# Moving the skip term between the weighted copies on ACT, with one decay semaphore per batch parity

## The chip, the core and the metric

The kernel runs on one core of a Trainium2 chip. PE (TensorE) does matmuls and transposes, DVE (VectorE) elementwise work and the scan, ACT (ScalarE) activations, POOL (GpSimd) elementwise work, and SP issues most DMAs. Each engine works through its own queue in order and waits for the others by semaphores. The metric is the device time of one execution in microseconds (us), lower is better.

## The reference

For 8 batches of 512 rows and 128 channels: a layer norm with a modulation from a condition, a Mamba block, a gated residual, a second layer norm, and a mixture of 8 experts (two of them weighted per row) beside a shared expert, with a second gated residual. Cut to what matters here:

```
mod = silu(c) @ wmod                                  # six vectors per batch
h = layernorm(x) * (1 + ca) + sa
xc, z = split(h @ in_proj.T);  xb = silu(conv4(xc) + conv_b)
dt, B, C = split(xb @ x_proj.T);  delta = softplus(dt @ dt_w.T + dt_b)
h[t] = h[t-1] * exp(delta[t] * A) + (delta[t] * xb[t]) * B[t]      # 16 states, 512 steps
y = (h * C).sum(states) + xb * D                      # xb * D is the skip term
x = x + ga * ((y * silu(z)) @ out_proj.T)
h = layernorm(x) * (1 + cb) + sb
x = x + gb * (shared(h) + sum_e w_e(h) * expert_e(h))  # w: softmax, top 2
```

## The kernel before

One batch is 256 inner channels (two groups q of 128 partitions) by 512 steps. The 16 states are cut into 16 units per batch (`UN`), each of one q and two states, so a unit is a tile of 128x1024 floats. For unit u of batch b:

- ACT `decays(b, u)` (L764 to L776): two activations exp(delta * A) into a ring of 8 decay tiles
- DVE `scan_input(b, u)` (L1067): B * du into PSUM, then `scan(b, u)` (L1076): the recurrence over 1024 columns into a ring of 4 states
- POOL `readout(b, u)` (L403): state * C. It is paced: it also waits for `input_done` of unit u + 1
- PE `y_add(b, u)` (L477): 8 transposes that accumulate the states into y in PSUM. Unit 15 is read out and added in the next slot, and so are the `y_add` of 13 and 14.

`pipeline` runs slots. In the slot of batch b, four batches are in work: b in its scans, a = b - 1 in its tail (gate, output projection, second norm, experts), n = b + 1 in its head (convolution, projections, delta), m = b + 2 in its first norm. The setup slot is the one with n = 0 and no b and a. Each engine has a function `slots(b, a, n, m)` whose order of calls is its queue.

What stands around the change in a slot with all four:

- DVE: after the scan of unit 7, `make_delta(n)` (L1040 to L1049) finishes delta and counts `delta_done`. After the scan of unit 12, `delta_x(n)` (L1056) makes `du` = xb * delta in place over xb. It waits for `skip_done`, because the skip term reads xb from the same tile. Behind it stand the scan inputs of units 13, 14 and 15, and in the next slot `gate_y` (L1086), `residual` and `split_h2` (L1180, `h_lo`).
- ACT: after the gelus of the experts (L903), `softplus_log(n)` (L846), the decays of b's unit 8, then a loop over j = 0 to 6: the decays of b's unit 9 + j, at j = 4 and 5 the decays of n's units 0 and 1, at j = 6 `h_rows(m)` (L784), and the weighted copies `mix_scaled(a, j)` (L869, four activations from PSUM). Then n's decays of unit 2, `mix_scaled(a, 7)`, `acc_rows(a)` (L876), `skip_term(n)` (L804, two activations, D * xb) and n's decays of units 3 to 5. After that comes the next slot, with the convolution's silu (L795).
- PE: `down(a, j)` (L633) and `mix_add(a, j)` (L643) alternate with b's `y_add`; `mix_add(a, j)` waits for the copy j. After `mix_add(a, 7)` come `y_add(b, 12)`, `acc_transpose(a)` (L652), and in the next slot `conv_in(n, 0)` (L504), `y_add` 13, `conv_in(n, 1)`, `y_add` 14 and 15, `x_proj`, `g_transpose`.

In the setup slot ACT ends with `z_gate(0)` (L813), for which PE's next `conv_in` waits.

`scan(b, u)` waits until the one semaphore `decay_done` has reached 16 b + u + 1. In ACT's order the decays of n's units 0 and 1 stand ahead of b's units 14 and 15, and count on the same semaphore.

Of the kernel before, what the change touches and what calls it, by code (L numbers as in the profile page):

```python
# [39 lines left out]
UN = 2 * CH  # L40
# [20 lines left out]
def adaln_mamba_moe_kernel(nc, x, in_proj_w, conv_w, conv_b, x_proj_w, dt_w, dt_b, a_log, d_skip,  # L61
# [4 lines left out]
    with ExitStack() as ctx:  # L66
# [3 lines left out]
        def sem(name):  # L70
            return ctx.enter_context(nc.semaphore(name))
# [128 lines left out]
        skip_done = sem("skip_done")  # L200
        du_done = sem("du_done")

        decay_done = sem("decay_done")
        input_done = sem("input_done")
        scan_done = sem("scan_done")
        read_done = sem("readout_done")
# [43 lines left out]
        def units_after(b, u):  # L250

            return b.i * UN + (u + 1)

        def unit(u):

            return u // (2 * Q), (u // 2) % Q, NU * (u % 2)
# [467 lines left out]
        def _(act):  # L724
# [19 lines left out]
            def load_silu_table(n):  # L744


                if not (isinstance(n.i, int) and n.i == 0):
                    act.wait_ge(silu_table, n.i)
                nc.scalar.activation(table_scratch[:, 0:1], eps_tile[:, 0:1],
                                     ACT.Silu).then_inc(silu_table, 1)  # L750
# [13 lines left out]
            def decays(b, u):  # L764

                pair, q, first = unit(u)
                r = u % DECAY_RING
                if u == 0:
                    act.wait_ge(delta_done, Q * b.i + Q)
                if not (isinstance(b.i, int) and b.i == 0 and u < DECAY_RING):  # L770
                    act.wait_ge(scan_done, units_after(b, u - DECAY_RING))
                for s in range(NU):
                    k = pair * NG + first + s
                    last = nc.scalar.activation(decay[:, r, s, 1:L], delta[:, b.p, q, 1:L], ACT.Exp,  # L774
                                                scale=a_neg[:, q, k:k + 1])
                last.then_inc(decay_done, 1)  # L776

            def h_rows(n):
                act.wait_ge(xT_done, n.i + 1)
# [8 lines left out]
            def x_silu(n, q):  # L788
                if q == 0 and not (isinstance(n.i, int) and n.i < 2):

                    act.wait_ge(input_done, (n.i - 1) * UN)
                if q == 0 and n.i == 0:
                    act.wait_ge(set_ev, EV_VEC)
                act.wait_ge(conv_done, Q * n.i + q + 1)
                nc.scalar.activation(du[:, n.p, q, :], A[q], ACT.Silu,  # L795
                                     bias=vec[:, ROW_CONVB + q:ROW_CONVB + q + 1]
                                     ).then_inc(xb_done, 1)

            def skip_term(n):

                act.wait_ge(delta_done, Q * n.i + Q)
                for q in range(Q):
                    act.wait_ge(xb_done, Q * n.i + q + 1)
                    nc.scalar.activation(skip[:, q, :], du[:, n.p, q, :], ACT.Identity,  # L804
                                         scale=vec[:, ROW_D + q:ROW_D + q + 1]).then_inc(skip_done, 1)

            def z_gate(n):
                if not (isinstance(n.i, int) and n.i < 2):
                    act.wait_ge(gT_done, n.i - 1)
                zs = z_silu[:, n.p, :, :].rearrange("p t c -> p (t c)")  # L810
                for j in range(2):
                    act.wait_ge(z_done, 2 * n.i + j + 1)
                    nc.scalar.activation(zs[:, j * 512:(j + 1) * 512], A[j],  # L813
                                         ACT.Silu).then_inc(zs_done, 1)

            def bcdt_rows(n):
                act.wait_ge(xproj_done, n.i + 1)
                if not (isinstance(n.i, int) and n.i == 0):
                    act.wait_ge(bc_stored, n.i * 16)
                    act.wait_ge(dt_done, Q * n.i)  # L820
                nc.scalar.activation(bcdt[:, :], MISC[0:2 * NS + R, :], ACT.Copy).then_inc(bcdt_done, 1)

            def softplus_relu(n, q):
                act.wait_ge(dt_done, Q * n.i + q + 1)
                nc.scalar.activation(delta[:, n.p, q, :], A[q], ACT.Relu,
                                     bias=vec[:, ROW_DTB + q:ROW_DTB + q + 1]).then_inc(sp_relu, 1)

            def softplus_abs(n, q, b):
                if b:
                    act.wait_ge(skip_acc, b.i + 1)  # L830
                act.wait_ge(dt_done, Q * n.i + q + 1)
                nc.scalar.activation(skip[:, q, :], A[q], ACT.Abs,
                                     bias=vec[:, ROW_DTB + q:ROW_DTB + q + 1]).then_inc(sp_abs, 1)

            def softplus_exp(n, a):
                act.wait_ge(sp_abs, Q * n.i + Q)
                if a:
                    act.wait_ge(oproj_done, a.i + 1)
                elif n.i > 0:
                    act.wait_ge(delta_done, Q * n.i)  # L840
                nc.scalar.activation(g_soft[:, :, :], skip[:, :, :], ACT.Exp,
                                     scale=-1.0).then_inc(sp_exp, 1)
# [6 lines left out]
            def g_rows(a, n):  # L849
                act.wait_ge(g_tr, a.i + 1)  # L850
                act.wait_ge(delta_done, Q * a.i + 2 * Q if n or isinstance(a.i, int) and a.i < B - 1
                            else Q * B)
                nc.scalar.activation(g_soft[:, :, :].rearrange("p q t -> p (q t)"), G_ROWS,
                                     ACT.Copy).then_inc(g_done, 1)

            def att_rows(a):
                act.wait_ge(oproj_done, a.i + 1)
                nc.scalar.activation(turned[:, :], OUTP, ACT.Copy,
                                     scale=gateT[:, 0, bass.ds(a.i, 1)]).then_inc(att_done, 1)
# [46 lines left out]
            def slots(b, a, n, m):  # L906
                if n:
                    load_silu_table(n)
                    x_silu(n, 0)
                    x_silu(n, 1)  # L910
                    bcdt_rows(n)
                if a:
                    g_rows(a, n)
                    att_rows(a)
                for q in range(Q):
                    if n:
                        softplus_relu(n, q)
                        softplus_abs(n, q, b)
                if n and n.i > 0:
                    z_gate(n)  # L920
                if n:
                    softplus_exp(n, a)
                if a:
                    load_exp_table(a)
                    h2_rows(a)
                if b:
                    decays(b, AHEAD)
                    decays(b, AHEAD + 1)
                if a:
                    router_e(a)  # L930
                    load_gelu_table(a)
                    for k in range(M_UP):
                        gelu(a, k)
                    weights_out(a)
                if n:
                    softplus_log(n)
                if b:
                    decays(b, AHEAD + 2)
                for j in range(DOWNS - 1):
                    if b:  # L940
                        decays(b, AHEAD + 3 + j)
                    if n and j in (4, 5):
                        decays(n, j - 4)
                    if m and j == 6:
                        h_rows(m)
                    if a:
                        mix_scaled(a, j)
                if n:
                    decays(n, 2)
                if a:  # L950
                    mix_scaled(a, DOWNS - 1)
                    acc_rows(a)
                if n:
                    skip_term(n)
                    for u in range(3, AHEAD):
                        decays(n, u)
                    if n.i == 0:
                        z_gate(n)

            pipeline(act, slots, setup)  # L960


        @block.vector
        def _(dve):
# [104 lines left out]
                                        ALU.mult).then_inc(input_done, 1)  # L1069

            def scan(b, u):
                dve.wait_ge(decay_done, units_after(b, u))
                if not (isinstance(b.i, int) and b.i == 0 and u < STATE_RING):
                    dve.wait_ge(yacc_done, units_after(b, u - STATE_RING))
                dve.wait_ge(input_done, units_after(b, u))
                nc.vector.tensor_tensor_scan(  # L1076
                    state[:, u % STATE_RING, :, :].rearrange("p n t -> p (n t)"),
                    decay[:, u % DECAY_RING, :, :].rearrange("p n t -> p (n t)"),
                    IN.rearrange("p n t -> p (n t)"), 0.0, ALU.mult, ALU.add).then_inc(scan_done, 1)
# [194 lines left out]
```

## Time and profile before

| | us |
|---|---|
| median of 3 runs | 754.61 |
| lowest, highest | 753.71, 760.47 |
| profiled execution | 761.24 |
| its span, first to last instruction | 759.5 |
| mean granted TensorE clock in it | 0.891 |
| busy PE, DVE, ACT, POOL | 625.6, 589.6, 497.0, 322.5 |

The profiled execution is a single one and lies at the upper end of the three timed runs. All rows below are of it. A row of a timeline gives the start and the duration in us, the engine and line, the output and inputs, and how many like instructions it holds. In square brackets stand the idle time of the engine ahead of it and what ended that. Starts of merged neighbours can overlap a little, since an engine begins an instruction before the last one has fully drained. A granted clock of 1.00 is full speed (2.4 GHz), 0.50 is half (1.2 GHz).

### The profile page before, as it was taken

What the parts mean: (1) busy time and instruction counts of PE and PEld (TensorE: products, weight loads), DVE (VectorE), ACT (ScalarE), POOL (GpSimd) and SP (SyncE); (2) the same over time, 40 slices, a digit from 0 to 9 for tenths busy, and PEclk for the clock granted to TensorE, in tenths of its full rate; (3) what the DMA queues carried; (4) which work ended last, traced back from release to release, by engine and by line L of the source; (5) the groups of instructions that cost most, each with busy time, mean ns of one, the idle gap of its engine ahead of it and who ended that gap; (6) DMA issues with size and microseconds to landing.
All of it is one profiled execution on the core that took longest, in us unless ns stands there. A gap on an engine that the chain in (4) does not pass through costs nothing.

```text
span 759.5 us, 9754 instructions
## 1 busy us (share of the span) xinstructions
PE 625.6 (82%) x3662; PEld 490.2 (65%) x3662; DVE 589.6 (78%) x669; ACT 497.0 (65%) x893; POOL 322.5 (42%) x172
## 2 busy tenths in 40 slices
PE   6547369997899969996999969996999758996897
PEld 4214245877477945885577936795487747795776
DVE  4477999796989969896989788996988699794300
ACT  3557643899278954898288945897289904871363
POOL 1025455353644635443543545443534464563000
PEclk9868559999799989998899989997999957997599
DMA  6503334133431325123421423231422343210000
GB/s 199 224 1 128 110 139 169 57 110 113 138 129 57 112 81 186 55 112 112 154 113 55 157 90 134 80 123 76 148 105 95 128 138 112 81 46 15 0 1 15
DMA packets 26369, 77.80 MB, mean 102 GB/s; under 512 B 2817, under 2 KB 17234, under 8 KB 18130
## 3 DMA queue, kind: packets, MB, share of 16 engines
q1 hardware_dynamic: 25842, 76.75, 27.9%
q8 instruction: 29, 0.48, 0.2%
q10 hardware_dynamic: 480, 0.43, 0.2%
q14 instruction: 18, 0.15, 0.1%
HBM read 74.55 MB, written 2.62 MB: 102 GB/s over the span
## 4 chain that ended last, share of the span: by engine, by line
PE 58%; ACT 23%; DVE 9%; issue 5%; POOL 3%; DMA 1%; POOLq 0%; DVEq 0%; ACTq 0%
PE psum L477 11%; PE psum L633 11%; PE psum L504 8%; ACT decay L774 6%; ACT gT_mix L869 4%; PE psum L601 4%; DVE state L1076 3%; PE psum L602 3%; PE psum L603 3%; POOL state L403 3%; ACT h L903 3%; DVE psum L1067 3%; PE psum L643 2%; PE psum L549 2%; PE psum L528 2%
## 5 line engine op out<-in xcount | busy, mean ns | idle before, releaser
L403 POOL TENSOR_TENSOR state<-state,bc 128x1024 f32<-128x1024 f32 x128 | 302.4, 2363 | 355.8 <-DVE psum L1067 354.8
L1076 DVE TENSOR_TENSOR_SCAN state<-decay,psum 128x1024 f32<-128x1024 f32 x128 | 292.2, 2283 | 19.5 <-PE psum L477 4.2
L477 PE MATMUL psum<-ident,state 128*128 128x128 f32 x1024 | 149.3, 296 | 73.2 <-POOL state L403 73.2
L477 PEld LDWEIGHTS psum<-ident,state 128*128 128x128 f32 x1024 | 129.2, 153 | 94.9 <-POOL state L403 81.3
L774 ACT ACTIVATE decay<-delta,a_neg 128x511 f32<-128x511 f32 x256 | 167.1, 728 | 30.7 <-DVE state L1076 28.5
L1067 DVE TENSOR_TENSOR psum<-bc,du 128x1024 f32<-128x1024 f32 x128 | 157.6, 1231 | 5.0 <-DVE state L1076 0.5
L633 PE MATMUL psum<-down_w,h 128*128 128x128 f32 x1024 | 125.3, 276 | 0.0
L633 PEld LDWEIGHTS psum<-down_w,h 128*128 128x128 f32 x1024 | 119.2, 192 | 6.1 <-issue 6.1
L903 ACT ACTIVATE h<-psum,vec 128x512 f32<-128x512 f32 x144 | 97.0, 688 | 15.6 <-PE psum L603 14.2
L869 ACT ACTIVATE gT_mix<-psum,w 128x128 f32<-128x128 f32 x256 | 74.0, 387 | 25.0 <-PE psum L643 17.6
L504 PE MATMUL psum<-h_sb,conv_in_wT 128*128 128x512 f32 x128 | 66.5, 671 | 17.0 <-ACT z_silu L813 17.0
L601 PE MATMUL psum<-h_hi,up_hi 128*128 128x512 f32 x144 | 61.5, 427 | 2.2 <-ACT h L903 1.3
L602 PE MATMUL psum<-h_lo,up_hi 128*128 128x512 f32 x144 | 58.3, 405 | 0.0
L603 PE MATMUL psum<-h_hi,up_lo 128*128 128x512 f32 x144 | 58.3, 405 | 0.0
L504 PEld LDWEIGHTS psum<-h_sb,conv_in_wT 128*128 128x128 f32 x128 | 27.3, 224 | 46.9 <-issue 46.8
L795 ACT ACTIVATE du<-psum,vec 128x512 f32<-128x512 f32 x16 | 11.0, 689 | 63.7 <-PE psum L504 63.7
L1056 DVE TENSOR_TENSOR du<-du,delta 128x1024 f32<-128x1024 f32 x8 | 9.8, 1222 | 39.6 <-ACT skip L804 39.6
L643 PE MATMUL psum<-ident,gT_mix 128*128 128x128 f32 x256 | 38.7, 274 | 1.9 <-ACT gT_mix L869 1.3
L601 PEld LDWEIGHTS psum<-h_hi,up_hi 128*128 128x128 f32 x144 | 28.0, 195 | 9.7 <-ACT h L903 2.8
L603 PEld LDWEIGHTS psum<-h_hi,up_lo 128*128 128x128 f32 x144 | 28.0, 194 | 6.9
L643 PEld LDWEIGHTS psum<-ident,gT_mix 128*128 128x128 f32 x256 | 29.8, 142 | 3.7 <-ACT gT_mix L869 3.7
L602 PEld LDWEIGHTS psum<-h_lo,up_hi 128*128 128x128 f32 x144 | 28.2, 196 | 5.5
(137 smaller groups left out, 633.1 us busy)
## 6 DMA issues: line engine op xcount, KB each, us to landing
bc<-bc_rows SPq DMA_DIRECT2D x64, 1024.0 KB, 4.7
x_sb<-_attn_hidden_states_dram SPq DMA_DIRECT2D x9, 256.0 KB, 2.8
out_dram<-out_sb SPq DMA_DIRECT2D x8, 256.0 KB, 2.4
x<-_attn_hidden_states_dram SPq DMA_DIRECT2D x7, 256.0 KB, 3.1
h<-in_L_ffn_rw_dram SPq DMA_DIRECT2D x1, 1024.0 KB
bc_rows<-rows SPq DMA_DIRECT2D x8, 64.0 KB, 1.6
h<-in_L_wmod_dram ACTq DMA_DIRECT2D x1, 384.0 KB
h<-in_L_attn_in_proj_w_dram SPq DMA_DIRECT2D x1, 256.0 KB, 4.4
```

Source lines behind the costliest of these rows:

```text
L403: pool.tensor_tensor(state[:, u % STATE_RING, :, :], state[:, u % STATE_RING, :, :], bc[:, pair % BC_RING, 1, first:first + NU, :], ALU.mu ...
L477: last = nc.tensor.matmul(Y[q][:, t * P:(t + 1) * P], state[:, u % STATE_RING, s, t * P:(t + 1) * P], ident[:, :], start=False, stop=(u in ...
L504: last = nc.tensor.matmul(A[q], conv_in_wT[:, q, k, :], h_sb[:, k:k + L], start=(k == 0), stop=(k == KC - 1))
L601: nc.tensor.matmul(bank, high, h2_hi[:, :], start=True, stop=False)
L602: nc.tensor.matmul(bank, high, h2_lo[:, :], start=False, stop=False)
L603: nc.tensor.matmul(bank, low, h2_hi[:, :], start=False, stop=True).then_inc(up_done, 1)
L633: last = nc.tensor.matmul(A[j % 2][:, e * DM:(e + 1) * DM], h1[:, (group * EG + e) * HQ + q, ts], down_w[:, group * EG + e, q, :], start=( ...
L774: last = nc.scalar.activation(decay[:, r, s, 1:L], delta[:, b.p, q, 1:L], ACT.Exp, scale=a_neg[:, q, k:k + 1])
L869: last = nc.scalar.activation(mix[:, j % 2, e, :], A[j % 2][:, e * DM:(e + 1) * DM], ACT.Copy, scale=w9[:, t, group * EG + e:group * EG + ...
L903: nc.scalar.activation(h1[:, m, :], UP_RING[m % 3], ACT.Gelu, bias=vec[:, bias:bias + 1]).then_inc(gelu_done, 1)
L1067: nc.vector.tensor_tensor(IN, bc[:, pair % BC_RING, 0, first:first + NU, :], du[:, b.p, q:q + 1, :].broadcast_to([P, NU, L]), ALU.mult).th ...
L1076: nc.vector.tensor_tensor_scan(state[:, u % STATE_RING, :, :].rearrange("p n t -> p (n t)"), decay[:, u % DECAY_RING, :, :].rearrange("p n ...
```

## The change

`skip_term(n)` is called in the loop at j = 3, behind the decays of b's unit 12 and ahead of `mix_scaled(a, 3)`, and no longer behind `acc_rows(a)`. There are two decay semaphores, chosen by the parity of the batch, and `scan(b, u)` waits on its own batch's for (b // 2) * 16 + u + 1. Nothing else differs.

```
-        decay_done = sem("decay_done")
+        decay_done = [sem(f"decay_done{p}") for p in range(2)]
...
-                last.then_inc(decay_done, 1)
+                last.then_inc(decay_done[b.p], 1)
...
                 for j in range(DOWNS - 1):
                     if b:
                         decays(b, AHEAD + 3 + j)
+                    if n and j == 3:
+                        skip_term(n)
                     if n and j in (4, 5):
                         decays(n, j - 4)
...
                     acc_rows(a)
                 if n:
-                    skip_term(n)
                     for u in range(3, AHEAD):
                         decays(n, u)
...
             def scan(b, u):
-                dve.wait_ge(decay_done, units_after(b, u))
+                dve.wait_ge(decay_done[b.p], (b.i // 2) * UN + u + 1)
```

ACT's queue in the first slot that has a tail (b = 1), from the decays of unit 11 on, before:

```order
L774 ACTIVATE decay<-delta,a_neg 128x511 x2
L869 ACTIVATE gT_mix<-psum,w 128x128 x4
L774 ACTIVATE decay<-delta,a_neg 128x511 x2
L869 ACTIVATE gT_mix<-psum,w 128x128 x4
L774 ACTIVATE decay<-delta,a_neg 128x511 x4
L869 ACTIVATE gT_mix<-psum,w 128x128 x4
```

and with the change:

```order
L774 ACTIVATE decay<-delta,a_neg 128x511 x2
L869 ACTIVATE gT_mix<-psum,w 128x128 x4
L774 ACTIVATE decay<-delta,a_neg 128x511 x2
L804 ACTIVATE skip<-du,vec 128x512 x2
L869 ACTIVATE gT_mix<-psum,w 128x128 x4
L774 ACTIVATE decay<-delta,a_neg 128x511 x4
L869 ACTIVATE gT_mix<-psum,w 128x128 x4
```

Here `gT_mix` is the tile of the weighted copies. The two skip activations now stand between the decays of unit 12 and the fourth copy; at the slot's end, behind `acc_rows` (L876), they are gone.

ACT's queue in the setup slot (batch 0), from the softplus logarithm to the z gate, before and with the change:

```order
 L846 ACT_TABLE_LOAD
 L846 ACTIVATE skip<-g_soft 128x1024
-L774 ACT_TABLE_LOAD
-L774 ACTIVATE decay<-delta,a_neg 128x511 x4
-L784 ACTIVATE h_sb<-psum,modT 128x512
-L774 ACTIVATE decay<-delta,a_neg 128x511 x2
-L804 ACTIVATE skip<-du,vec 128x512 x2
-L774 ACTIVATE decay<-delta,a_neg 128x511 x6
+L804 ACTIVATE skip<-du,vec 128x512 x2
+L774 ACT_TABLE_LOAD
+L774 ACTIVATE decay<-delta,a_neg 128x511 x4
+L784 ACTIVATE h_sb<-psum,modT 128x512
+L774 ACTIVATE decay<-delta,a_neg 128x511 x8
 L813 ACT_TABLE_LOAD
 L813 ACTIVATE z_silu<-psum 128x512 x2
```

The skip term stands first now, ahead of the load of the table for Exp.

## Rows read from the trace of the kernel before

**Rows 1.** The page: busy time of each engine (share of the span), instructions
```profile
PE 625.6 (82%) x3662; PEld 490.2 (65%) x3662; DVE 589.6 (78%) x669; ACT 497.0 (65%) x893; POOL 322.5 (42%) x172
```

**Rows 2.** Waits of DVE: us in total, times, longest us
```profile
DVE du L1056 <- ACT skip L804: 39.6, 7, 5.8
```

**Rows 3.** Timeline of DVE: setup, steady slots 1, 3, 4 and 6
```profile
42.50 1.23 DVE L1056 TENSOR_TENSOR du<-du,delta 128x1024 f32<-128x1024 f32 x1 [5.83 <-ACT skip L804]
...
187.60 1.23 DVE L1056 TENSOR_TENSOR du<-du,delta 128x1024 f32<-128x1024 f32 x1 [5.62 <-ACT skip L804]
...
329.33 1.29 DVE L1049 TENSOR_TENSOR delta<-delta,skip 128x512 f32<-128x512 f32 x2
...
347.07 2.29 DVE L1076 TENSOR_TENSOR_SCAN state<-decay,psum 128x1024 f32<-128x1024 f32 x1
355.00 1.23 DVE L1056 TENSOR_TENSOR du<-du,delta 128x1024 f32<-128x1024 f32 x1 [5.63 <-ACT skip L804]
...
373.70 1.23 DVE L1086 TENSOR_TENSOR gT_mix<-psum,z_silu 128x1024 f32<-128x1024 f32 x1 [1.12 <-PE psum L477]
...
390.35 1.17 DVE L1180 TENSOR_TENSOR h_lo<-h,h_hi 128x512 fp32r<-128x512 f32 x1 [1.82 <-ACT h_hi L884]
...
439.01 1.23 DVE L1056 TENSOR_TENSOR du<-du,delta 128x1024 f32<-128x1024 f32 x1 [5.71 <-ACT skip L804]
...
605.57 1.23 DVE L1056 TENSOR_TENSOR du<-du,delta 128x1024 f32<-128x1024 f32 x1 [5.39 <-ACT skip L804]
```

**Rows 4.** Timeline of POOL: readouts of units 12 and 15 of one batch
```profile
357.50 2.34 POOL L403 TENSOR_TENSOR state<-state,bc 128x1024 f32<-128x1024 f32 x1 [8.11 <-DVE psum L1067]
...
368.97 2.35 POOL L403 TENSOR_TENSOR state<-state,bc 128x1024 f32<-128x1024 f32 x1 [1.80 <-DVE psum L1067]
```

**Rows 5.** Timeline of PE: another slot's convolution, then 324 to 437
```profile
279.22 4.08 PE L504 MATMUL psum<-h_sb,conv_in_wT 128*128 128x512 f32 x8
...
324.74 1.95 PE L618 MATMUL psum<-h,down_w 128*128 128x512 f32 x4 [1.04 <-ACT rows L896]
...
359.89 1.97 PE L477 MATMUL psum<-ident,state 128*128 128x128 f32 x8 [6.97 <-POOL state L403]
...
362.51 5.10 PE L504 MATMUL psum<-h_sb,conv_in_wT 128*128 128x512 f32 x8
367.45 1.03 PE L477 MATMUL psum<-ident,state 128*128 128x128 f32 x8
368.32 3.60 PE L504 MATMUL psum<-h_sb,conv_in_wT 128*128 128x512 f32 x8
...
435.54 1.40 PE L643 MATMUL psum<-ident,gT_mix 128*128 128x128 f32 x8
```

**Rows 6.** Windows: length, busy PE, PEld, DVE, ACT, POOL, clock, DMA share, GB/s
```profile
299.00:354.00 55.00, 51.81 (x370) 45.45 (x368) 46.12 (x62) 50.04 (x95) 24.91 (x14) 1.00 0.30 114
...
359.80:362.60 2.80, 2.71 (x13) 2.71 (x14) 2.65 (x2) 2.75 (x4) 1.51 (x2) 0.50 0.00 0
362.60:367.70 5.10, 5.10 (x12) 2.22 (x12) 4.93 (x5) 0.07 (x1) 3.24 (x2) 0.71 0.23 62
```

**Rows 7.** Timeline of ACT: decays of unit 12, copy j = 3, skip
```profile
336.60 1.34 ACT L774 ACTIVATE decay<-delta,a_neg 128x511 f32<-128x511 f32 x2
338.96 1.14 ACT L869 ACTIVATE gT_mix<-psum,w 128x128 f32<-128x128 f32 x4 [1.01 <-PE psum L643]
...
353.54 1.32 ACT L804 ACTIVATE skip<-du,vec 128x512 f32<-128x512 f32 x2
```

**Rows 8.** Timelines of ACT, PE and DVE in the setup slot and behind it
```profile
33.29 1.28 ACT L774 ACT_TABLE_LOAD   x1
36.70 2.55 ACT L774 ACTIVATE decay<-delta,a_neg 128x511 f32<-128x511 f32 x4 [2.12 <-DVE delta L1049]
...
48.57 8.55 PE L504 MATMUL psum<-h_sb,conv_in_wT 128*128 128x512 f32 x16 [17.02 <-ACT z_silu L813]
...
63.87 2.29 DVE L1076 TENSOR_TENSOR_SCAN state<-decay,psum 128x1024 f32<-128x1024 f32 x1 [4.17 <-PE psum L477]
```

## Prediction of the changed kernel's time

> **What bounds the kernel now.** I began with the page's busy times [rows 1]: PE is busy 82% of the span, DVE 78%. Neither is full, so waits in a ring between engines must set the time. A steady slot of the batch pipeline repeats every 83.6 us, from (605.57 - 187.60) / 5 for the first and the last steady `du` multiply [rows 3]. The question is which wait ends last in a slot, so I read DVE's waits [rows 2]. The largest is `du` at L1056, which waits for ACT's skip term, 39.6 us in 7 waits. One of them (5.83 us, at 42.50) lies in the setup slot. The other six, 33.8 us in all or 5.6 each, lie in slots 1 to 6 [rows 2, 3].
>
> Then I followed one slot through the timelines. On DVE the scan of unit 12 ends at 349.36, `du` starts at 355.00 [rows 3]. On POOL, the readout of unit 12 is paced by the scan input of unit 13, which stands behind `du` on DVE, so it starts only at 357.50 [rows 4]. On PE it idles 6.97 us for that readout, until 359.89, so its last `mix_add` had ended at 352.92 [rows 5]. Behind this stand the transposed accumulation of unit 12, the transpose of the expert rows and both convolutions of the next batch. So the whole ring goes mix on PE, `acc_rows` and skip on ACT, `du` and the input on DVE, readout on POOL, PE again. The skip term is on it, although its inputs are old: the delta steps end at 330.62 [rows 3], and skip starts at 353.54 [rows 7]. Nothing but its place in ACT's queue makes it late.
>
> **What the change moves.** In a steady slot the two skip activations (1.32 us) go from behind `acc_rows` to behind the decays of unit 12, ahead of the fourth weighted copy (j = 3). Those decays end at 337.94; the delta steps, for which skip waits, had ended at 330.62, 7.3 us before. So skip runs at about 337.9 to 339.2 and `du`, ready at 349.37, waits for nothing. That takes 5.6 us off DVE's ring per slot.
>
> What it costs on ACT: the fourth copy started at 338.96 after 1.01 us of idle [rows 7]. Skip needs 1.2 to 1.3 us there (neighbours overlap by 0.1), so the copies behind are late by 0.2 to 0.3 us. From there to the end of the slot ACT's queue is full, and the delay reaches the last `mix_add`. PE then idles that much less ahead of unit 12, which is free as long as PE still has to wait there (below).
>
> **The new ring.** DVE from one `du` to being ready for the next: (439.01 - 5.71) - 355.00 = 78.30 us, and this contains waits for PE and ACT: 1.12 at the gate, 1.82 at `h_lo` [rows 3]. PE from the start of unit 12 to the end of its last `mix_add`: 436.94 - 359.89 = 77.05 [rows 5], plus 0.3 for the moved skip. The two rings meet at unit 12: PE may start it when the last `mix_add` has ended and when the readout has, which follows `du` by a fixed 4.9 us (355.00 to 359.86 [rows 3, 4]). Both are under 83.6, and DVE's is the longer by 78.30 - 77.35 = 0.95 us. So the next bound is DVE's ring, and PE still waits at unit 12, for about 1 us in place of 7.
>
> That shorter idle matters by itself. In the idle of 7 us the granted clock falls: it is 0.50 over 359.8 to 362.6, when PE works again, and comes back only during 362.6 to 367.7, whose mean is 0.71 [rows 6]. The work in between runs at half speed: 8 transposes 1.97 us against 1.03 at full clock, the first convolution 5.10 us (4.08 in another slot) against 3.60 [rows 5]. An idle of 1.04 us in the middle of a slot (ahead of 324.74) left the clock at 1.00 over the whole of 299 to 354 [rows 5, 6]. With about 1 us of idle I expect it to stay at its upper level, 2.4 GHz, so that the first convolution takes 3.6 us. PE could then save 3 us, but it gets less: unit 15 needs its readout, which is tied to DVE and ends at 371.32, 11.43 us after PE's unit 12 starts [rows 4, 5]. With 0.9 us of transposes it ends 12.35 us after, against 373.67 - 359.89 = 13.78 now (the gate at 373.70 starts on it [rows 3]). So 1.4 us. The gate's wait of 1.12 goes, and the rest shows at `h_lo`. DVE's ring becomes 78.30 - 1.4 = 76.9. In the slots where the convolution took only 4.08 us the ring was shorter already by about as much, so they end near 77 as well.
>
> On this clock the Trainium skill (TensorE: Matmul & The Clock Gate, Part 1) says that the clock gate is at 4/8 after idling and 8/8 after sustained work, which is the 0.50 and 1.00 of the trace. Its warning that the change-over varies from run to run agrees with the first convolution's 4.08 and 5.10 us; by that rule alone a part of the gain could be missing in some slots, which is the first rival below.
>
> **The setup slot pays.** For batch 0 the order on ACT was table load (33.29, while ACT waited for the delta steps), decays, skip, decays, table load, z gate. Now skip is first and waits for delta; the built order has the Exp table load behind it. The load of 1.28 us no longer lies in the wait that ends at 36.70, and all of ACT's work behind it, up to the z gate, comes 1.3 us later [rows 8]. PE's second convolution waits 17.02 us for that gate, and DVE's scan at 63.87 waits 4.17 us for PE [rows 8], so this 1.3 us is on the path. DVE gets its `du` sooner there (42.50 now [rows 3]), which only lengthens that wait. Beside it, the Trainium skill (ScalarE: Activation LUTs, Table sets) says that cheap functions are in every table set, so Identity needs no load of its own; the built order agrees, as in it no load stands ahead of skip, before or now.
>
> In slot 0 `du` waited for nothing. Skip will wait there for the delta steps and hold back the decays of unit 13, which are needed some 20 us later: nothing.
>
> The second edit, one decay semaphore per parity, adds no instruction. In the old count the decays of the next batch's units 0 and 1 counted for units 14 and 15 of this one; now the scan waits for the true ones. Unit 15's decays stand ahead of the old skip at 353.54 in ACT's queue, so with the 1.3 us of the moved skip they have ended by 354.9 at the latest [rows 7]. Unit 15's scan in the new order has `du`, three inputs and two scans ahead of it from 349.4 on, 1.2 + 3 x 1.2 + 2 x 2.3 = 9.4 us, so it starts at 358.8 or later [rows 3]: a margin of 4 us at least, so nothing.
>
> **The sum.** Slot 1: 5.6. Five rings at 83.6 - 76.95 = 6.65: 33.2. Setup: -1.3. Slot 7 and the tail: no convolution stands there, and a gain from the clock lies between 0 and 1.5 us; I take nothing. Together 37.5 us. The profiled execution has 761.24 us (span 759.5), so 723.7 on its own ground. It lies 6.6 us over the median of 754.61, and on the median's ground that would be 717.1. The first convolution's duration, 4.08 us in one slot and 5.10 in another [rows 5], is a kind of spread that the new order removes: over six slots up to 6 us. I count about half of the 6.6 as such. So about 720.5.
>
> **Rivals.**
> - *The clock still falls.* For: it fell in the idle of 7 us [rows 6], and my 1 us is the small difference of two long rings. Against: the 1.04 us idle did not do it. Then the gain is that of the waits alone, 33.8 - 1.3 = 32.5: 728.7 on the profile's ground, 722 on the median's.
> - *ACT stalls at the new place* (the other side). If the delta steps end later than the decays of unit 12, skip blocks the copies j = 3 to 7, the decays of 13 to 15 and `h_rows` behind it, and PE behind those. Now the margin is 7.3 us. A lateness beyond it would first eat PE's 1 us of idle and then 1:1 each slot. If the delta steps come L us later against ACT than now, the time is 720.5 + 6 x (L - 8.3): 747 us (1% under before) at L = 12.7, 762 us (1% over) at 15.2. For it: DVE becomes the bounding engine. Against: the delta steps and ACT's decays both hang on the same scans, so they move together.
> - *The change does nothing*: excluded if the trace is right, since `du` names skip as its last releaser in all seven waits, and the built order has moved it.
>
> **Numbers.** A measurement of this kernel can tell about 1% (7.5 us) from no change. My forecast 0.77, the clock falling 0.13: both are faster by over 1%, 0.90. ACT stalls so that 1% is not reached 0.06; slower by over 1% 0.04. The range goes from 714 (the median's ground with 1.5 us at the tail and 1.5 for the rest) to 729 (waits alone on the profile's ground).
>
> **What would show it.** DVE `du` has no wait for skip in slots 1 to 6; skip starts before the fourth copy; PE's idle ahead of unit 12 is 0.5 to 1.5 us, its releaser still POOL; the granted clock at the first convolution is 1.00 and it takes 3.6 us; `du` repeats every 77 us; the z gate of setup is 1.3 us later. It would be wrong if PE's idle has gone and the ring is over 78 us (then ACT's copies bound it), or if ACT waits for the delta steps ahead of skip in steady slots.

## The result, and the profile after

The changed kernel takes 724.47 us (median of 4, 722.56 to 725.67), beside 755.97 for the kernel before (753.71 to 760.47). The medians lie 31.5 us apart. The ratio, taken from the means, is 0.957, with a 95% interval of 0.952 to 0.963, so 4.3% less. The profiled execution took 722.56 us, with a span of 720.8 and a mean granted clock of 0.930 (0.891 before).

The page's first part, its chain by engine, and the waits of DVE (us in total, times, longest), where [rows 1, 2] stood:

```profile
PE 608.0 (84%) x3662; PEld 475.5 (66%) x3662; DVE 587.9 (82%) x669; ACT 495.3 (69%) x893; POOL 322.4 (45%) x172
...
DVE 38%; PE 36%; ACT 12%; issue 7%; POOL 5%; DMA 1%; DVEq 0%; POOLq 0%; ACTq 0%
```

```profile
DVE h_lo L1181 <- ACT h_hi L884: 17.4, 8, 3.5
...
DVE du L1057 <- ACT skip L804: 1.5, 1, 1.5
```

The 39.6 us that `du` waited for skip are 1.5 us, all in the setup slot. DVE is now the largest engine on the chain, where PE was before (58%, DVE 9%). Of the timelines, one slot of DVE, POOL and PE, and two rows of ACT from the slot behind it, the answers to [rows 3, 4, 5, 7]:

```profile
334.01 2.29 DVE L1077 TENSOR_TENSOR_SCAN state<-decay,psum 128x1024 f32<-128x1024 f32 x1
336.22 1.20 DVE L1057 TENSOR_TENSOR du<-du,delta 128x1024 f32<-128x1024 f32 x1
...
338.69 2.35 POOL L403 TENSOR_TENSOR state<-state,bc 128x1024 f32<-128x1024 f32 x1 [2.37 <-DVE psum L1068]
...
341.09 1.09 PE L477 MATMUL psum<-ident,state 128*128 128x128 f32 x8 [1.14 <-POOL state L403]
342.02 0.60 PE L652 MATMUL psum<-ident,h 128*128 128x128 f32 x4
342.46 3.60 PE L504 MATMUL psum<-h_sb,conv_in_wT 128*128 128x512 f32 x8
...
352.58 1.09 PE L477 MATMUL psum<-ident,state 128*128 128x128 f32 x8 [1.33 <-POOL state L403]
...
402.13 1.34 ACT L804 ACTIVATE skip<-du,vec 128x512 f32<-128x512 f32 x2
403.36 1.14 ACT L869 ACTIVATE gT_mix<-psum,w 128x128 f32<-128x128 f32 x4
```

`du` follows the scan of unit 12 at once. PE idles 1.14 us ahead of unit 12 where it idled 6.97, and the first convolution takes 3.60 us. So the slot looks as forecast. But not every slot does. Two steady slots have a longer wait at `h_lo`, 3.46 and 3.31 us in place of 1.83. The timelines of DVE and PE and two windows (length, busy PE, PEld, DVE, ACT, POOL, granted clock, DMA share, GB/s) show the first of them:

```profile
208.80 2.70 PE L512 MATMUL psum<-z_wT,h_sb 128*128 128x256 f32 x8
...
286.63 1.89 PE L512 MATMUL psum<-z_wT,h_sb 128*128 128x256 f32 x8
...
215.96 0.69 DVE L1181 TENSOR_TENSOR h_lo<-h,h_hi 128x512 fp32r<-128x512 f32 x1 [3.46 <-ACT h_hi L884]
...
195.00:206.00 11.00, 8.66 (x42) 4.38 (x39) 10.76 (x7) 2.88 (x5) 6.18 (x3) 1.00 0.43 149
206.00:210.00 4.00, 4.00 (x14) 3.05 (x14) 3.81 (x12) 2.04 (x4) 3.52 (x3) 0.63 0.82 305
```

The granted clock falls in the middle of the slot: it is 1.00 up to 207 us and 0.50 over 207 to 210, and PE is busy in all of those 3 us. The fall comes just behind the two dt projections (L528, matmuls that contract 8 rows). `z_proj` (L512) takes 2.70 us in this slot and 3.21 in the other, in place of 1.89, and its silu, `h_hi` and `h_lo` follow late. I call this a dip below.

Where the 38.7 us between the two profiled spans (759.5 and 720.8) lie, by the starts of `du`: the first steady one came at 187.60 and comes at 180.19, 7.4 us sooner; five rings fell from 417.97 to 388.49 us (to 568.68), 29.5 us; the rest fell from 153.9 to 152.1 us. The medians, 31.5 us apart, are less apart than the two profiles; the part on the prediction comes back to this.

### The profile page after: what moved, and what is told of

Same layout as the page of the kernel before. It is cut to its first block, busy times and chain, and to the rows that moved or that the text cites. A ratio compares the mean times of both kernels' runs of the same rounds, so it can differ in the third digit from the quotient of the medians.

```text
span 720.8 us, 9754 instructions
## 1 busy us (share of the span) xinstructions
PE 608.0 (84%) x3662; PEld 475.5 (66%) x3662; DVE 587.9 (82%) x669; ACT 495.3 (69%) x893; POOL 322.4 (45%) x172
## 4 chain that ended last, share of the span: by engine, by line
DVE 38%; PE 36%; ACT 12%; issue 7%; POOL 5%; DMA 1%; DVEq 0%; POOLq 0%; ACTq 0%
DVE state L1077 17%; DVE psum L1068 12%; PE psum L633 6%; PE psum L477 6%; POOL state L403 4%; PE psum L504 3%; PE psum L549 2%; ACT h L903 2%; PE psum L528 2%; PE psum L522 2%; PE psum L512 2%; ACT decay L774 2%; PE psum L601 2%; PE psum L542 1%; PE psum L603 1%
## 5 line engine op out<-in xcount | busy, mean ns | idle before, releaser
L477 PE MATMUL psum<-ident,state 128*128 128x128 f32 x1024 | 145.7, 290 | 45.6 <-POOL state L403 45.6
L477 PEld LDWEIGHTS psum<-ident,state 128*128 128x128 f32 x1024 | 125.0, 150 | 68.4 <-POOL state L403 52.8
L504 PE MATMUL psum<-h_sb,conv_in_wT 128*128 128x512 f32 x128 | 60.3, 617 | 18.7 <-ACT z_silu L813 18.7
L504 PEld LDWEIGHTS psum<-h_sb,conv_in_wT 128*128 128x128 f32 x128 | 24.4, 200 | 44.6 <-issue 44.6
L643 PE MATMUL psum<-ident,gT_mix 128*128 128x128 f32 x256 | 38.7, 274 | 3.8 <-ACT gT_mix L869 3.8
L795 ACT ACTIVATE du<-psum,vec 128x512 f32<-128x512 f32 x16 | 11.0, 688 | 39.6 <-PE psum L504 39.6
L853 ACT ACTIVATE g_soft<-psum 128x1024 f32<-128x1024 f32 x8 | 8.2, 1028 | 32.4 <-PE psum L542 32.4
```

Of the source, the lines that this page charges most:

```text
L477: last = nc.tensor.matmul(Y[q][:, t * P:(t + 1) * P], state[:, u % STATE_RING, s, t * P:(t + 1) * P], ident[:, :], start=False, stop=(u in ...
L504: last = nc.tensor.matmul(A[q], conv_in_wT[:, q, k, :], h_sb[:, k:k + L], start=(k == 0), stop=(k == KC - 1))
```

## The experiments

All timings are medians, and a ratio is to the kernel before as timed beside that run. For each profile I read the five rings of `du`, from the first to the last steady slot, and the dips in six steady slots (a `z_proj` over 2.5 us, or where that isn't read, `h_lo` waiting over 3.2 us):

| kernel | us | mean ring | dips of 6 |
|---|---|---|---|
| before | 755 to 760 | 83.59 | 1 |
| changed | 724.47 | 77.70 | 2 |
| changed, again | 724.85 | 77.69 | 2 |
| semaphores alone | 755.84 | 83.29 | 0 |
| setup order kept | 722.05 | 77.68 | 2 |
| skip ahead of acc_rows | 748.24 | 81.87 | 0 |
| before, 50 transposes in the idle | 758.72 | 83.77 | 4 |
| before, unit 12 unpaced | 762.37 | 83.82 | 3 |
| setup kept, short idles filled | 724.24 | 78.35 | 4 |
| skip's work twice | 724.88 | 77.66 | 2 |
| 8 transposes between the dt projections | 725.44 | 77.90 | 0 |
| 8 transposes ahead of them | 727.83 | 78.58 | 2 |
| unit 0 between them | 722.80 | 77.62 | 0 |
| 3 transposes between them | 720.29 | 77.35 | 0 |

The first eight runs were to tell apart two theories, A and B, that both say that the waits carry the gain, and differ on what the clock adds.

### The changed kernel again

> The changed kernel once more, as the yardstick of this group. The two theories are: (A) the six removed waits of du for the skip term carry the gain (5.6 us each, 33.8 us less 1.3 us in the setup slot), and TensorE's clock adds up to 1 us per slot; (B) the waits alone carry it, the clock gives nothing on balance, since a dip that went from the first convolution can come back elsewhere in the slot. Both expect 722 to 726 us here; A expects rings of du of 77.0 us where no stretch of the slot lies at half clock, B expects a mean ring of 78 us.

Measured 724.85 us, ratio 0.957 (0.952 to 0.961) to its own kernel before, mean ring 77.69, with dips in slots 5 and 6 (in slots 2 and 6 the first time). The rings without a dip are 77.0 (one is 77.4), as A has it; the mean is near that of B.

### The semaphores alone

```
-        decay_done = sem("decay_done")
+        decay_done = [sem(f"decay_done{p}") for p in range(2)]
-                last.then_inc(decay_done, 1)
+                last.then_inc(decay_done[b.p], 1)
-                dve.wait_ge(decay_done, units_after(b, u))
+                dve.wait_ge(decay_done[b.p], (b.i // 2) * UN + u + 1)
```

> The kernel before with the second edit alone, two decay semaphores by the batch's parity. Both theories: no instruction is added and unit 15's decays have long ended when its scan starts, so the time is that of the kernel before within 0.5% (752 to 759 us), and du still waits 5.6 us for skip in six slots. A theory by which the semaphores matter (the scan waits longer for the true decays, or less because the counts are separate) expects more than 5 us of difference.

Measured 755.84 us beside 756.16, ratio 1.000 (0.996 to 1.004). The second edit costs and brings nothing in time that this can tell, 0.4% either way. The move alone on the one semaphore was not tried, because it would have a race: decays of the next batch count for unit 14 before unit 14's own are written. In the kernel before, `du` waited for the skip term, which stands behind all decays of the batch on ACT, and this wait was what ordered the scans of units 14 and 15 behind their decays. The move takes that order away, so it needs the second edit.

### Batch 0's skip term at its old place

```
-                    if n and j == 3:
+                    if n and a and j == 3:
                         skip_term(n)
...
                 if n:
+                    if not a:
+                        skip_term(n)
                     for u in range(3, AHEAD):
```

> The changed kernel, but batch 0's skip term in the setup slot stands at its old place, behind the decays. If the Exp table load behind the moved skip (1.28 us) is on the path there, the z gate comes 1.3 to 1.4 us earlier against the delta steps than in the changed kernel, and the time falls by about 1.3 us, 0.2%, which a profile shows better than the times. If that stretch is covered, the time is the same and DVE waits as long for PE at its first stall.

ACT's timeline in the setup slot, first of the changed kernel, then of this one:

```profile
35.81 1.33 ACT L804 ACTIVATE skip<-du,vec 128x512 f32<-128x512 f32 x2 [3.42 <-DVE delta L1050]
37.16 1.28 ACT L774 ACT_TABLE_LOAD   x1
38.46 2.56 ACT L774 ACTIVATE decay<-delta,a_neg 128x511 f32<-128x511 f32 x4
...
46.59 1.28 ACT L813 ACT_TABLE_LOAD   x1
```

```profile
32.76 1.28 ACT L774 ACT_TABLE_LOAD   x1
36.16 2.55 ACT L774 ACTIVATE decay<-delta,a_neg 128x511 f32<-128x511 f32 x4 [2.12 <-DVE delta L1052]
...
45.51 1.28 ACT L813 ACT_TABLE_LOAD   x1
```

From the end of the delta steps (the first activation behind the wait) to the z gate's load it is 46.59 - 35.81 = 10.78 us in the changed kernel and 45.51 - 36.16 = 9.35 here: 1.4 us, the load in the open. The time, 722.05 beside 724.85, points the same way, but single runs of either spread over 4 us, so the 1.4 rests on the profile. How much of it reaches the end is open: behind the gate, PE's convolution takes 9.23 us in one profile and 9.78 in the other. The Trainium skill (ScalarE: Activation LUTs, What ACT_TABLE_LOAD costs) gives a load about 1.28 us and a drain of about 1.38 beside it. The load of 1.28 is what the rows show; the drain is not to be seen here, since the decays start 1.30 us after the load does (37.16 and 38.46).

### The skip term one step earlier only

```
-                    if n and j == 3:
-                        skip_term(n)
...
                 if a:
                     mix_scaled(a, DOWNS - 1)
+                if n:
+                    skip_term(n)
+                if a:
                     acc_rows(a)
```

> The changed kernel with the skip term between the last weighted copy and acc_rows, so only 1.4 us earlier than in the kernel before. It asks whether the time follows the skip term's place 1:1. If the ring through du bounds (A and B), du waits about 4.1 us in place of 5.6, each of six slots is 1.4 to 1.5 us shorter, and with the setup slot's 1.3 us the time is 755 - 8.7 + 1.3 = 748 us (745 to 751). If the gain came from taking ACT's work out of the end of the slot, it would be that of the kernel before; if any place ahead of acc_rows does, 724.

Its waits of DVE:

```profile
DVE du L1058 <- ACT skip L804: 30.9, 7, 5.8
```

Less the setup slot's 5.8 us that is 25.1 us in six slots, 4.2 each (5.6 before). The time is 748.24 beside 756.16, ratio 0.988 (0.985 to 0.992): 7.9 us. The wait fell by 8.7 us. I had added 1.3 us for the setup slot wrongly: in this kernel batch 0's order is the old one. The ring through `du` follows the place of the skip term nearly 1:1, which a gain from mere rearrangement at the end of the slot would not.

### PE's idle filled, skip left where it was

```
+                    if a and b and n and u == UN - 3:
+                        fill(a, 50)
                     if b:
                         y_add(b, u - 1)
```

> The kernel before, with 50 transposes of the identity on PE in its idle of 7 us ahead of unit 12's accumulation (their result is never used); skip stays where it was. It measures the clock by itself. By A the first convolution takes 3.6 us in all slots, PE reaches unit 15 as early as POOL allows, and the ring of du falls from 83.6 to about 82.6, so 6 us in all (747 to 751 us). By B the clock falls elsewhere in the slot in its place, and the time is that of the kernel before within 2 us.

Rows of its PE timeline:

```profile
268.23 5.62 PE L573 MATMUL psum<-ident 128*128 128x128 f32 x50
275.37 1.09 PE L477 MATMUL psum<-ident,state 128*128 128x128 f32 x8 [1.52 <-POOL state L403]
...
276.74 3.60 PE L504 MATMUL psum<-h_sb,conv_in_wT 128*128 128x512 f32 x8
...
299.08 2.75 PE L512 MATMUL psum<-z_wT,h_sb 128*128 128x256 f32 x8
```

The first part of A came true: the convolution takes 3.60 us, and rings without a dip are 82.8 us (187.66 to 270.47, 439.76 to 522.60), where 82.6 was expected. But in that same slot the clock then fells `z_proj`. Four of six steady slots dip, a ring with one is 83.9 to 84.8, and the mean is 83.77. The time is 758.72, ratio 1.001 (0.998 to 1.005): nothing gained, as B says (it is 2.3 us over the 756.38 beside it, where B allowed 2). In the kernel before, five of six steady slots had no dip, nor had any in the two other kernels whose clock falls at the start of each slot. So here a clock kept up at the start of the slot went with more dips some 20 us later. That the one brings the other is not shown: in slot 1 of both this kernel and the one before, the first convolution is slow (5.70 and 5.63 us) and the slot dips all the same.

### PE's idle taken away, skip left where it was

```
-                        readout(b, u)
+                        readout(b, u, paced=u != 12)
```

> The kernel before, with the readout of unit 12 no longer paced by the scan input of unit 13, so that POOL needn't wait for du; skip stays. It takes away PE's idle but not du's wait. By A and B the ring through du and skip hangs on PE's mix chain, so PE's 7 us are gone, the next accumulation (unit 13) waits for its readout instead, and the time falls only by what the clock and the earlier first convolution give, 1 to 2 us per slot (745 to 752 us). If PE's idle of 7 us were the cost by itself, this would bring most of the gain: 720 to 730 us.

```profile
357.40 1.04 PE L477 MATMUL psum<-ident,state 128*128 128x128 f32 x8
...
358.84 3.60 PE L504 MATMUL psum<-h_sb,conv_in_wT 128*128 128x512 f32 x8
368.17 1.97 PE L477 MATMUL psum<-ident,state 128*128 128x128 f32 x8 [5.73 <-POOL state L403]
369.93 5.39 PE L504 MATMUL psum<-h_sb,conv_in_wT 128*128 128x512 f32 x8
```

Unit 12 no longer waits; the idle stands one unit later, 5.73 us, the clock falls there, and now the second convolution is the slow one. 762.37 us, ratio 1.006 (1.003 to 1.010), so 6 us worse and not 4 to 11 better. The small gain I expected failed: the mean ring is 83.82, with three dips. These stand in slots whose second convolution was slow, so a fall early in the slot does not keep a later one away. In slot 0 there is a further cost, since the unpaced readout now runs beside a scan input on DVE:

```profile
106.71 3.37 DVE L1067 TENSOR_TENSOR psum<-bc,du 128x1024 f32<-128x1024 f32 x1
```

It takes 3.37 us in place of 1.23, and POOL's two readouts there take 5.66 in place of 2 x 2.34. The rest of the 6 us I didn't trace. That PE's idle by itself was not what cost the time is shown by both runs.

### The skip term's work twice

```
                     if n and j == 3:
+                        if a:
+                            (two activations, D * xb into a tile of their own, 496 columns each)
                         skip_term(n)
```

> The changed kernel with two more activations like the skip term (1.2 us, into a tile that nothing reads) right ahead of it in the slots with copies. PE has 1.1 us of idle left ahead of unit 12. If DVE's ring bounds the changed kernel, as forecast, ACT's added 1.2 us is eaten by that idle and the ring of du stays at 77.0 to 77.3 us: at most 2 us more in all. If ACT's copies bound it, the ring grows by 1.2 us in each of six slots: 7 us more.

```profile
326.28 1.31 ACT L949 ACTIVATE twin<-du,vec 128x496 f32<-128x496 f32 x2
327.48 1.34 ACT L806 ACTIVATE skip<-du,vec 128x512 f32<-128x512 f32 x2
...
341.99 0.65 PE L645 MATMUL psum<-ident,gT_mix 128*128 128x128 f32 x4 [1.37 <-ACT gT_mix L871]
342.63 1.09 PE L479 MATMUL psum<-ident,state 128*128 128x128 f32 x8
```

724.88 us, the time of the changed kernel, rings of 77.0 without a dip. The last copy comes later, and PE's idle ahead of unit 12 is used up. So ACT has 1.2 us to spare there, and it is DVE's ring that bounds the changed kernel. With PE's idle used up, one more microsecond on ACT in this stretch should be paid; that was not run.

### The short idles filled

The kernel of setup order kept, with 7, 9 and 5 transposes ahead of unit 12, of unit 15 and of `g_transpose`.

> The changed kernel with batch 0's skip at its old place, and with 7, 9 and 5 transposes of the identity in PE's three short idles of a slot (ahead of units 12 and 15 and of g_transpose; results never used). By A the dips of the clock in the middle of two slots go, all five rings of du are 77.0 us, and the time is 1.3 + 3 us under the changed kernel: 719 to 721 us. By B the dips have another cause and stay, and the time is that of the changed kernel less 1.3 us: 722 to 724 us.

724.24 us (719.57 to 727.79), four dips, mean ring 78.35. It is a miss for A. More work on PE in the idle places did not keep the clock up where it falls. This left open what precedes the fall. In the dips it comes at the end of the second dt projection or just behind it, so the next two runs put the same 8 transposes at two places around them.

### Eight transposes between the dt projections, and ahead of them

```
                 if a:
                     out_proj(a)
+                (ahead: fill(1, 8) here)
                 if n:
                     dt_proj(n, 0)
                 if a:
                     att_transpose(a)
+                (between: fill(1, 8) here)
                 if n:
                     dt_proj(n, 1)
```

> The e3 kernel (batch 0's skip at its old place) with 8 transposes of the identity on PE between the two dt projections, whose matmuls contract only 8 rows; the granted clock has fallen right behind them in some slots. It costs PE 0.9 us on its way to h_hi. By C (the fall hangs on what PE does there) no slot dips, h_lo never waits 3.3 us or more beyond the 0.9, and all rings of du are alike, 77.0 to 77.9 us. By B' (the fall hangs on something else, a matter of chance at that place) 2 to 4 of six slots still dip, and the time is 1 to 5 us over e3's.

> The control to it: the same 8 transposes ahead of the first dt projection, so the same 0.9 us at nearly the same place, with the two dt projections as close together as before. By C dips stay in 2 to 4 of six slots; by B' this and the run with the transposes between the projections are alike.

Between: no dip in six steady slots, rings of 77.6 to 78.2 us (C had said up to 77.9), times within 1.1 us of each other (724.50 to 725.60). Ahead: two dips, 727.83 us. Same work, same number of instructions, same cost of 0.9 us on the way to `h_hi`; only the place differs. None of six against two of six is thin by itself, and the next two runs add to it. Windows of the run with them ahead, from 1.2 us before `z_proj` in a slot with a dip, and of the run with 3 between (below), from the start of `z_proj`:

```profile
287.00:291.00 4.00, 4.00 (x16) 3.50 (x15) 3.96 (x13) 1.76 (x3) 1.57 (x3) 0.57 0.38 147
```

```profile
286.00:290.00 4.00, 4.00 (x31) 3.69 (x30) 4.00 (x6) 3.08 (x5) 1.32 (x3) 1.00 0.39 160
```

PE counts as busy for all of both windows, and the clock is 0.57 in one and 1.00 in the other. Nor is it the DMA traffic at this step, an obvious rival: its share is up to 1.02 in 1 us of the first, but in the run with 3 between it is 0.93 and 1.01 over 285 to 287, with the clock at 1.00.

### Needed work between them, and a smaller dose

The first moves `y_add(b, 0)` from behind the second dt projection to ahead of it; the second is the run with 8 transposes between, with 3.

> The e3 kernel with PE's accumulation of unit 0 (8 full transposes, needed work) moved from behind the second dt projection to between the two. By C, which the two runs with 8 transposes between and ahead of the projections bore out, no steady slot dips: z_proj takes 1.89 us in all. The second projection is 0.9 us later and half of that is covered by ACT, so rings of du are 77.4 to 77.6 us, and the time is 719.5 to 722. If only added transposes help, z_proj takes 2.7 us or more in some slots.

> As the run with 8 transposes between the dt projections, but 3. It asks how much is needed. By C with a small dose: no dips, rings of du 77.3 us, 719 to 721 us. If 3 are too few, some slots show z_proj at 2.7 us or more and the time is e3's, 722 to 724 us.

```profile
283.07 0.66 PE L556 MATMUL psum<-ident,h 128*128 128x128 f32 x4
283.56 0.49 PE L573 MATMUL psum<-ident 128*128 128x128 f32 x3
283.99 1.12 PE L528 MATMUL psum<-rows,small_w 8*128 8x512 f32 x2
285.04 1.09 PE L477 MATMUL psum<-ident,state 128*128 128x128 f32 x8
285.97 1.89 PE L512 MATMUL psum<-z_wT,h_sb 128*128 128x256 f32 x8
```

No dip in either. With unit 0 between, 722.80 us, 0.8 over what was expected: its rings of 77.6 us carry 0.6 us for the later second projection, and that eats what the dips had cost. With 3 transposes, rings of 77.3 and 720.29 us (719.67 to 722.69), ratio 0.952 (0.947 to 0.957): the fastest kernel here, 4 us under the changed one by the medians. More than half of that is not the transposes': the kernel that it is built on, with the setup order kept, has 722.05, so 1.8 us are left, and the single runs of the two overlap (719.67 to 722.69, 719.49 to 724.00). What is clear is in the rings, 77.35 on the mean beside 77.68. Taken together, 0 of 18 steady slots dip in the three profiles with transposes between the projections, and 18 of 42 in the seven others whose convolutions run at the full clock from the second steady slot on (the changed kernel twice, setup kept, the 50 transposes, short idles filled, skip twice, 8 ahead). The first steady slot has a slow first convolution in all ten; without it the counts are 0 of 15 and 17 of 35. There is one profile of each run, and the slots of one profile need not be independent.

## Why the prediction was right, and where it was off

It said 720.5 us, within 714 to 729, faster; measured were 724.5. By its steps:

- **The ring and its weakest wait**: right. Six waits of 5.6 us have gone; a move of one step brought the share of that step (7.9 us for 8.7 us of wait); the idle of PE, taken away or filled, brought nothing.
- **The cost on ACT, free as long as PE waits**: right, and shown with twice the work. The fourth copy stands right behind skip (403.36 behind 402.13), PE's idle is 1.14 us, forecast at about 1.
- **The next bound is DVE's ring**: right. Rings without a dip are 76.7 to 77.4 us, two of them 77.01 (336.22 to 413.23 is one), forecast 76.9.
- **The setup slot pays 1.3 us**: right by ACT's timeline, 1.4; its share in the time is not shown.
- **The semaphores cost nothing**: right in time. That the move needs them was not said.
- **The clock stays up, and brings 1.4 us per ring**: this is the term that was mis-sized. It stays up at the first convolution in the steady slots from the second on (3.60 us), as said, and the first rival, by which it falls there still, is wrong on the place. On the time, 722 on the median's ground, that rival is nearer than the forecast. But it falls later in two of the steady slots, which the prediction did not see: 5 x (83.59 - 76.95) = 33.2 us was the term, and the rings gave 29.5. A dip costs 1.4 to 1.6 us (rings of 78.64 and 78.44 beside 77.01). The trace of before had one such place to see, a wait of 3.5 us at `h_lo` behind slot 0, which the prediction does not mention.
- **From the profile to the median**: the profiled execution lay 6.6 us over the median, and I moved by half of it. On the profile's own ground the sum said 723.7, and the span fell by 38.7 us for the 37.5 forecast. That closeness is partly luck: 3.1 us came in ahead of the first steady `du`, where before the first convolution took 5.63 us and a dip followed, and after it took 4.28 and none did, and 1.8 us in the tail; they made up for the 3.7 that the rings fell short.
- **The 6.6 us between profile and median**: this was misread. The medians fell by 31.5 us, which is near the rival's 32.5 (waits alone) and 6 us short of 37.5. The prediction took half of the 6.6 us as a spread that the new order removes. But the 45 timed runs of the kernel before beside the experiments fall into two groups, 29 of 753.4 to 757.1 us at a clock of 0.903 to 0.908 and 16 of 759.7 to 763.2 us at 0.889 to 0.891, and the profile is of the upper one. The semaphores alone left a profile of the lower group (span 752.8 us, clock 0.905, rings of 83.29 with the same waits for skip). Against that one the span of the changed kernel is 32.0 us shorter and its rings 5.6 us, which is the waits and nothing more. So on balance the clock has added little here, and the gain is that of the waits. This is worked out from sums and single profiles; what supports it is that filling the idle before the change moved the time by 0.1%, with an interval of 0.3% to either side. What sets the two groups apart was not looked into.

## What to carry to other kernels

When an engine waits in every slot for a term whose inputs are old, the place of that term in its engine's queue is the cost. Follow the whole ring to the next engine's idle time, then compute the next ring before moving it, as it says how much of the wait can be had: here all 5.6 us of it, with 1.1 us of PE's idle left over. Before a wait is removed, ask what it also ordered: here it kept two scans behind their decays. And where a clock is held up by one change, look along the rest of the slot for where it falls next; a comparison of rings with and without the fall tells more than the total.

## What the runs showed of the hardware

The granted clock of PE can fall to 0.50 while the records show PE busy without a gap (207 to 210 us of the changed kernel, 3.00 of 3.00 us busy). Here it did so behind two pairs of matmuls that contract 8 rows, with an `att_transpose` between, in 18 of 42 slots, and in none of 18 slots where 3 or 8 more transposes of 128 x 128 stood between the pairs (the 8 of `y_add`, needed work, did as well as idle ones). The Trainium skill (TensorE: Matmul & The Clock Gate, Part 1) says that the gate follows how busy PE has been; by the profile's busy time alone that isn't what these rows show, 4.00 of 4.00 us busy at 0.57 and at 1.00. What exactly is counted stays open, as does why only some slots fall.

Two tensor operations side by side on DVE and POOL can be slow together: DVE's scan input took 3.37 us beside POOL's readout where it takes 1.23 when they are paced apart. This was seen once, in slot 0 of the run with unit 12 unpaced.
